# Selection of the second token half moved beside the feed-forward products, in 28 pieces

## The reference, cut to what matters

```python
inter = xf @ c1_w.T @ c2_w.T                # (tokens, 1792), rank 16
blk = inter.reshape(B * T, 56, 32)
idx = argmax(blk, -1) + arange(0, 1792, 32) # one unit of each 32
h = relu(einsum('bkm,bm->bk', w1[idx], xf))
out = einsum('bk,bkm->bm', h, w2t[idx])
```

## Time and profile before

| | |
|---|---|
| median of 3 runs | 2140.83 us (2140.81 to 2145.97) |
| the profiled execution's own time | 2140.16 us |
| its span | 2138.4 us |
| TensorE busy | 2061.0 us (96%) |
| VectorE busy | 1596.8 us (75%) |
| ScalarE busy | 1447.9 us (68%) |
| GpSimd busy | 773.9 us (36%) |
| 16 DMA engines | 20.9% of the span for the main queue |

### The profile page before, as it was taken

One profiled execution on the slowest core, in us unless ns is written; L12 is line 12 of the kernel. 1 busy time (PEld: TensorE's weight loads), 2 busy tenths in 40 slices (PEclk: granted clock), 3 DMA queues, 4 the chain that ended last, 5 costly groups with the idle time before them and its releaser, 6 DMA issues. The chain is left out here.

```text
span 2138.4 us, 33991 instructions
## 1 busy us (share of the span) xinstructions
PE 2061.0 (96%) x12990; PEld 1662.1 (78%) x12990; DVE 1596.8 (75%) x1763; ACT 1447.9 (68%) x3141; POOL 773.9 (36%) x423
## 2 busy tenths in 40 slices
PE   6899999999999999999999999997899989999988
PEld 5788888888888888888888888884587668888864
DVE  6778788878877877887888787787623358787774
ACT  4777786777777678677677778782633357777761
POOL 2244444444354436434454434534444201010101
PEclk8999999999999999999999999997999999999999
DMA  3222232222222222122222212221132111010001
GB/s 110 106 88 91 78 109 72 77 101 78 99 80 103 76 81 107 70 99 79 74 100 101 83 69 99 86 92 33 59 116 88 42 44 30 22 30 22 14 1 40
DMA packets 56241, 157.46 MB, mean 74 GB/s; under 512 B 16656, under 2 KB 27152, under 8 KB 47632
## 3 DMA queue, kind: packets, MB, share of 16 engines
q1 hardware_dynamic: 56080, 155.28, 20.9%
HBM read 152.64 MB, written 2.62 MB: 73 GB/s over the span
## 5 line engine op out<-in xcount | busy, mean ns | idle before, releaser
L610 PE MATMUL PS<-xnh,wh 128*128 128x512 f32 x1272 | 509.8, 401 | 8.6 <-DVE xnl L1590 5.8
L612 PE MATMUL PS<-xnh,wl 128*128 128x512 f32 x1272 | 497.0, 391 | 0.0
L611 PE MATMUL PS<-xnl,wh 128*128 128x512 f32 x1272 | 496.1, 390 | 0.0
L1627 DVE SCALAR_TENSOR_TENSOR arena<-PS,arena 128x1020 f32<-128x1020 f32 (+2 forms) x240 | 305.6, 1274 | 31.1 <-ACT arena L1219 25.4
L1180 ACT ACTIVATE PS<-x,arena 128x128 f32<-128x128 f32 x1024 | 308.1, 356 | 21.1 <-DVE arena L1659 20.1
L610 PEld LDWEIGHTS PS<-xnh,wh 128*128 128x128 f32 x1272 | 239.2, 188 | 63.3 <-issue 14.3
L450 POOL TENSOR_TENSOR zl<-arena,zh 128x1024 fp32r<-128x1024 f32 x63 | 176.8, 2807 | 293.6 <-ACT zh L1202 293.6
L612 PEld LDWEIGHTS PS<-xnh,wl 128*128 128x128 f32 x1272 | 239.2, 188 | 52.0
L611 PEld LDWEIGHTS PS<-xnl,wh 128*128 128x128 f32 x1272 | 239.5, 188 | 46.1
L446 POOL TENSOR_TENSOR arena<-arena 128x1024 f32<-128x1024 f32 x63 | 151.9, 2412 | 297.9 <-ACT arena L1198 297.9
L435 POOL TENSOR_TENSOR wl<-arena,wh 128x1024 fp32r<-128x1024 f32 x72 | 174.8, 2428 | 199.5 <-ACT wh L1169 199.5
(11 more groups left out here) (253 smaller groups left out, 4123.9 us busy)
## 6 DMA issues: line engine op xcount, KB each, us to landing
x<-decay SPq DMA_DIRECT2D x64, 1024.0 KB, 4.6
arena<-in_w_xg SPq DMA_DIRECT2D x72, 512.0 KB, 5.5
arena<-in_w_o SPq DMA_DIRECT2D x32, 512.0 KB, 3.4
arena<-in_w_f SPq DMA_DIRECT2D x28, 512.0 KB, 3.5
x<-in_x SPq DMA_DIRECT2D x3, 1024.0 KB, 5.4
arena<-in_w_h SPq DMA_DIRECT2D x16, 192.0 KB, 2.9
arena<-in_w_h SPq DMA_DIRECT2D x16, 129.0 KB, 2.8
out<-x SPq DMA_DIRECT2D x8, 256.0 KB, 2.0
```

What stands on the lines that cost most here:

```text
L610: mm(PS[:, bank], ah, bh, start=(n == 0), stop=False)
L611: mm(PS[:, bank], ah, bl, start=False, stop=False)
L612: last = mm(PS[:, bank], al, bh, start=False, stop=(n == len(terms) - 1))
L1627: ins = stt(o, pair_of(bank).rearrange("p q (b t) -> p q b t", t=SEQ)[:, :, :, :SEQ - k], w[:, 3 - k:4 - k], o, ALU.mult, ALU.add)
```

## The change

Only the 8 selection steps of tokens 0 to 511 stay ahead of the feed-forward loop. The selection of tokens 512 to 1023 is cut into 28 pieces j of 128 tokens by 2 tiles (256 units), spread over iterations n = 0 to 14: TensorE does step(2n) between hidden(n + 1) and down(n), and step(2n + 1) behind down(n). One step holds the two score products of piece j, the first-maximum product of piece j-2 and the two turns of piece j-1, in banks T and S. The score weights move from zl to woh and wol, so zl is free for the loop. hidden(1) moves ahead of the last first_part, and down(0) waits for the 8 masks of the first half. The low part of the input's second half becomes four operations in iterations 4 to 7 on GpSimd. The head weights and four small constants are loaded together behind w_f of n = 17, after a wait for all 36 masks.

The diff without the score weights' new place and the waits on it:

```diff
 NF = 2 * FT1
+NPC = FT1 // 2 * NU // 2
...
-        c2r = zl.rearrange("p k t -> p (k t)")[:, 0:F1]
+        c2r = [v.rearrange("p k t -> p (k t)")[:, 0:F1 // 2] for v in (woh, wol)]
...
+        def piece(j):
+
+            return j // 4, NU // 2 + j % 4
+
...
-            for n in range(NF):
-                if n >= 2:
-                    sp.wait_ge(s["fw2l"], n - 1)
-                sp.dma_start(w_f[:, n % 2], d["w_f"][n % FT1]).then_inc(s[f"w_f{n % 2}"], 16)
+            for m in range(NF):
+                if m >= 2:
+                    sp.wait_ge(s["fw2l"], m - 1)
+                sp.dma_start(w_f[:, m % 2], d["w_f"][m % FT1]).then_inc(s[f"w_f{m % 2}"], 16)
+                n = m
                 if n == 5:
-                    sp.wait_ge(s["mT"], 2 * NU)
+                    sp.wait_ge(s["c1_ps"], 2)
+                    sp.wait_ge(s["c2_r"], 3)
                     for dst, name in ((w_qc, "w_qc"), (w_kvc, "w_kvc"), (bq, "bq"), (bkv, "bkv"), (bv, "bv"), (bo, "bo"), (w_oT, "w_oT")):
                         sp.dma_start(dst, d[name]).then_inc(s["a_in"], 16)
+                if n == FT1 + 3:
+                    sp.wait_ge(s["mT"], NU + NPC)
                     for n in range(2):
                         sp.dma_start(bqB[n * QB:(n + 1) * QB], d["bq"][0:QB]).then_inc(s["a_in"], 16)
                         sp.dma_start(bias_rows[n * NPAIR:(n + 1) * NPAIR], d["w_hB"][:, QB, n]).then_inc(s["a_in"], 16)
-                if n in (6, 7):
-                    heads_load(n - 6)
+                    for i in range(2):
+                        heads_load(i)
...
-                po.wait_ge(s["ln_h"], h + 3)
-                nc.gpsimd.tensor_tensor(xnl[:, :, half(h)], xn[:, :, half(h)], xnh[:, :, half(h)].bitcast(F32), ALU.subtract)\
-                    .then_inc(s["ln_l"], 1)
+            po.wait_ge(s["ln_h"], 3)
+            nc.gpsimd.tensor_tensor(xnl[:, :, half(0)], xn[:, :, half(0)], xnh[:, :, half(0)].bitcast(F32), ALU.subtract)\
+                .then_inc(s["ln_l"], 1)
...
+                if 4 <= n < 4 + KD:
+                    po.wait_ge(s["ln_h"], 4)
+                    k = n - 4
+                    last = nc.gpsimd.tensor_tensor(xnl[:, k, half(1)], xn[:, k, half(1)], xnh[:, k, half(1)].bitcast(F32), ALU.subtract)
+                    if k == KD - 1:
+                        last.then_inc(s["ln_l"], 1)
...
-            for v in range(2 * NU):
-                if v == 2 * NU - 1:
-                    pe.wait_ge(s["ln_l"], 4)
+            def step(j):
+
+                if j == 0:
+                    pe.wait_ge(s["eqT"], NU)
+                    pe.wait_ge(s["t1"], 3)
+                if j < NPC:
+                    f, u = piece(j)
+                    pe.wait_ge(s["eq"], NU + j)
+                    for n in range(2):
+                        q, at = divmod(2 * f + n, FT1 // 2)
+                        last = mm(PS[:, T, col(n)], t1[:, col(u)], c2r[q][:, col(at)], start=True, stop=True)
+                    last.then_inc(s["in_ps"], 1)
+                if 2 <= j < NPC + 2:
+                    pe.wait_ge(s["eqT"], NU + j - 1)
+                    pe.wait_ge(s["mT"], NU + j - 2)
+                    mm(PS[:, S, SEQ:], ahead, eqT[:, j % 2, 0:2], start=True, stop=True).then_inc(s["first_ps"], 1)
+                if 1 <= j < NPC + 1:
+                    pe.wait_ge(s["eq"], NU + j)
+                    pe.wait_ge(s["eqT"], NU + j - 1)
+                    for n in range(2):
+                        last = nc.tensor.transpose(PS[:, S].bitcast(BF16)[:, col(n)], eq[:, (j - 1) % 2, col(n)], identB[:, :])
+                    last.then_inc(s["eqT_ps"], 1)
+
+            for v in range(NU):
+                if v == NU - 1:
+                    pe.wait_ge(s["ln_l"], 3)
                     hidden(0)
                 turn_part(v)
-                if v + 2 < 2 * NU:
+                if v + 2 < NU:
                     in_part(v + 2)
                 if v == 0:
                     c1_part(1, Y0, range(2, KD))
                 if v:
                     first_part(v - 1)
-            first_part(2 * NU - 1)
+            hidden(1)
+            first_part(NU - 1)
 
             for n in range(NF):
-                if n + 1 < NF:
+                if n + 1 == FT1:
+                    pe.wait_ge(s["ln_l"], 4)
+                if 0 < n < NF - 1:
                     hidden(n + 1)
+                if n <= FT1:
+                    step(2 * n)
                 if n == 0:
-                    pe.wait_ge(s["mT"], 2 * NU)
+                    pe.wait_ge(s["mT"], NU)
                 if n == FT1 + 1:
                     pe.wait_ge(s["x2"], 1)
                     narrow(T, 2 * P, onesD, x, 0).then_inc(s["ln_mean"], 1)
@@ -899,6 +946,8 @@
                     pe.wait_ge(s["rows_w"], 3)
                     widen_pair(1, sdn[:, col(2)]).then_inc(s["ln_rw"], 1)
                 down(n)
+                if n <= FT1:
+                    step(2 * n + 1)
 
 
             def latent_A(h, bank):
@@ -1368,20 +1417,35 @@
                     ac.wait_ge(s[done], n - 1)
                 act(wh[:, k, c], w_f[:, k, c], ACT.Copy).then_inc(s["fw2h" if part else "fw1h"], 1)
 
-            for v in range(2 * NU):
+            def high_half(h):
+                ac.wait_ge(s["ln_xn"], h + 3)
+                act(xnh[:, :, half(h)], xn[:, :, half(h)], ACT.Copy).then_inc(s["ln_h"], 1)
+
+            def step(j):
+                if 1 <= j < NPC + 1:
+                    ac.wait_ge(s["eqT_ps"], NU + j)
+                    if j >= 3:
+                        ac.wait_ge(s["first_ps"], NU + j - 2)
+                    act(eqT[:, (j - 1) % 2, 0:2], PS[:, S].bitcast(BF16)[:, 0:SEQ].rearrange("p (c t) -> p c t", t=P), ACT.Copy)\
+                        .then_inc(s["eqT"], 1)
+                if 2 <= j < NPC + 2:
+                    f, u = piece(j - 2)
+                    ac.wait_ge(s["first_ps"], NU + j - 1)
+                    act(maskT[:, 2 * f:2 * f + 2, col(u)], PS[:, S, SEQ:].rearrange("p (c t) -> p c t", t=P), ACT.Relu)\
+                        .then_inc(s["mT"], 1)
+
+            for v in range(NU):
                 turned_part(v)
                 if v == 0:
                     t1_high(1, Y0)
                 if v:
                     mask_part(v - 1)
-                if v in (4, 8):
-                    h = v // 4 - 1
-                    ac.wait_ge(s["ln_xn"], h + 3)
-                    act(xnh[:, :, half(h)], xn[:, :, half(h)], ACT.Copy).then_inc(s["ln_h"], 1)
-                if v in (10, 12):
-                    rounded(v // 2 - 5, 0, "h_ps")
-                    rounded(v // 2 - 5, 1, "f_out")
-            mask_part(2 * NU - 1)
+                if v == 1:
+                    high_half(0)
+                if v in (3, 5):
+                    rounded(v // 2 - 1, 0, "h_ps")
+                    rounded(v // 2 - 1, 1, "f_out")
+            mask_part(NU - 1)
 
             for n in range(NF):
                 if 1 <= n < NF - 1:
@@ -1390,8 +1454,16 @@
                 if n >= 2:
                     ac.wait_ge(s["f_out"], n - 1)
                 act(zh[:, n % 2, 0:HALF], hs[:, n % 2], ACT.Copy).then_inc(s["hs_h"], 1)
+                if 1 <= n <= FT1:
+                    step(2 * n - 1)
+                if n == 2:
+                    high_half(1)
                 if 1 <= n < NF - 1:
                     rounded(n + 1, 1, "f_out")
+                if n <= FT1:
+                    step(2 * n)
+                if n == FT1:
+                    step(2 * n + 1)
                 if n == FT1 + 2:
                     mean(2, 0, T, 2 * P)
                 if n == FT1 + 5:
@@ -1825,14 +1897,31 @@
                 tt(eq[:, q].rearrange("p (b g i) -> p b g i", b=2, i=SP1), scores, across(top.unsqueeze(3), shape),
                    ALU.is_equal).then_inc(s["eq"], 1)
 
+            def step(j):
+                if j >= NPC:
+                    return
+                scores = PS[:, T, 0:SEQ].rearrange("p (g i) -> p g i", i=SP1)
+                top = mx[:, j % 2, 0:SEQ // SP1]
+                ve.wait_ge(s["in_ps"], NU + j + 1)
+                V.tensor_reduce(top, scores, AX_X, ALU.max).then_inc(s["mx"], 1)
+                ve.wait_ge(s["mx"], NU + j + 1)
+                ve.wait_ge(s["eqT_ps"], NU + max(j - 1, 0))
+                tt(eq[:, j % 2, 0:SEQ].rearrange("p (g i) -> p g i", i=SP1), scores, across(top.unsqueeze(2), (P, SEQ // SP1, SP1)),
+                   ALU.is_equal).then_inc(s["eq"], 1)
+
             for n in range(NF):
                 k, h = n % 2, n // FT1
                 ve.wait_ge(s["h_ps"], n + 1)
                 if n >= 2:
                     ve.wait_ge(s["hs_l"], n - 1)
+                ve.wait_ge(s["mT"], NU + (n - FT1) // 2 * 4 + 4 if h else NU)
                 stt(hs[:, k], PS[:, A + k], 0.0, maskT[:, n % FT1, half(h)], ALU.max, ALU.mult).then_inc(s["hs"], 1)
                 ve.wait_ge(s["hs_h"], n + 1)
                 tt(zl[:, k, 0:HALF], hs[:, k], zh[:, k, 0:HALF].bitcast(F32), ALU.subtract).then_inc(s["hs_l"], 1)
```

(4 more changed lines are left out.)

16 lines of the change are left out of this document (10 added, 6 removed).

## The result

The changed kernel takes 2149.08 us (median of 20 runs, 2143.98 to 2151.86) against 2143.01 us for the kernel before on the same chip (20 runs, 2140.03 to 2146.56). The ratio is 1.0025, 95% interval 1.0019 to 1.0031: 5.4 us slower, 4.1 to 6.6 (the medians lie 6.1 apart), and within the 0.3% (6.4 us) that the prediction called the same.

What follows compares the result with a forecast made beforehand. TensorE was taken to bound the feed-forward loop and VectorE the last selection steps; -17.0 + 1.5 + 11.4 + 1.0 + 2.7 + 3.4 = +3.0 us gave a median of 2143.8 us, range 2137 to 2152.

Steps and rivals of the forecast that it cites:

- The case that the text called likeliest: The forecast itself for the whole kernel: 2143.8 us, told as the same within 0.3%; chance 0.52.
- Eight steps: Selection ahead of the loop: eight steps of 2.13 us removed, so the first hidden product starts earlier, -17.0 us.
- Start of the loop: From the first hidden product to down(0): 10.0 us against 8.5, with 3.3 us of TensorE waiting, +1.5 us.
- Pieces: Between down(0) and down(13): 26 steps of small TensorE products at 0.44 us each, +11.4 us (8.8 to 15.6).
- The upper bound: Cost of one step: about 0.6 us, with a first product's delay of 0.14 at each of two operand changes.
- Weight chain: In the loop, from a step's end to the low part of hidden(n + 2)'s weights: 3.1 us, covered by 3.16, 0.
- The rival of 2152 us: In the loop: GpSimd's low part begins 0.69 us late, weight chain 3.8 against 3.16 us, 8 us slower; chance 0.15.
- VectorE's low part beside GpSimd's: At the shared SBUF port: VectorE's low part waits for GpSimd's, started 0.6 us earlier, with over 2 us of room.
- Change of halves: From down(13)'s end to down(14): step(28) waits for VectorE's comparison of piece 27, 5.6 us against 4.59, +1.0 us.
- End of iteration 14: Ahead of hidden(16): ScalarE writes the last mask before rounding tile 16's weights, so TensorE waits, +2.7 us.
- SyncE's burst: Head weight loads of 8.7 us ahead of tile 18's w_f: 0.4 us late unless TensorE is delayed, 0.
- Clock: Behind the new pauses of 3.3 and 2.6 us: 3.4 us at 1.2 GHz each, costing 1.7 each, +3.4 us.

Runs made afterwards that it cites:

- The first experiment: Changed kernel with ScalarE's rounding of tile 16's first weights ahead of the last piece's mask; ratio 1.0017 to the kernel before.
- the filled pause: Changed kernel with 12 wide products, whose result nobody reads, in TensorE's pause ahead of down(0); ratio 1.0025 to the kernel before.
- the kernel with the low part whole: Changed kernel with the second half's low part as one GpSimd operation in iteration 4 instead of four; ratio 1.0033 to the kernel before.
- the kernel with four repairs: Changed kernel with tile 16's rounding first, head weights' loads spread, last first maximum ahead of hidden(1), one score product in 24 pieces; ratios 1.0000 and 0.9992 to before.

## Why the prediction was right

The forecast was 2143.8 against 2140.83, +3.0 us; it came to +5.4 (4.1 to 6.6) timed and +4.2 in the part of the trace that the change touches. The case that the text called likeliest is the one that happened, with its marks: the first down 15.9 us earlier, counted from the start of selection (15.5 forecast); idle of 3.12 us ahead of it, ended by the low part; an iteration of 6.47 us (6.3 forecast); hidden(16) released by GpSimd 2.6 us late; 3.4 us at half clock behind both; no idle TensorE time between steady iterations.

- **Eight steps**, -17.0: -17.7. The last eight steps before took 17.03 us, as the eight periods say; the other 0.65 is in the eight that stay (1487.72 to 1506.84, 19.12 us, against 18.47), and why was not looked into. It makes up for a part of what the pieces cost beyond the forecast; that is luck.
- **Start of the loop**, +1.5: +1.8; undoing its order gave 1.1 of it back.
- **Pieces**, +11.4 at 0.44: the mis-sized term, 13.2 at 0.51. The products' own spacings are less than forecast: 0.18 + 0.12 + 0.08 = 0.38 us. What the sum lacked is the 0.09 us that the first wide product behind a step takes longer, and the 0.004 us on each of the eleven others. The upper bound had the first of these, "the delay of a first product, 0.53 against 0.39 us", at two places of 0.14; it is one of 0.09. The kernel without pieces shows that all of it is theirs.
- **Weight chain**, 0, on a cover of 0.06 us: right, with 0.47 of room in fact, so the chain was sized 0.4 us too long. ScalarE's copy, mask and rounding start 0.28 and 0.26 us apart (1604.87, 1605.15, 1605.41), where I had taken 0.43 for each. The rival of 2152 us needs 0.5 us more in the chain than there is.
- **VectorE's low part beside GpSimd's**, predicted to be late and hidden: 1.14 us at 1593.89 instead of 0.69, ending 0.55 us behind GpSimd's operation from 1593.19 to 1594.48, and nobody waits for it. The rule of the Trainium skill that the prediction weighed (SBUF — State Buffer, "SBUF: two separate sides") agrees with this row.
- **Change of halves**, +1.0: +0.8. **End of iteration 14**, +2.7: +2.6, and 4.15 us came back, its clock with it, once two orders were mended.
- **SyncE's burst**, 0: right in the kernel after, and only because the end's pause hides it. The first experiment and the kernel without pieces show the wait (3.27 and 1.83 us).
- **Clock**, +3.4: right in both places, 1.7 us each; the filled pause shows the cause for the first. The argument was that each pause is longer than one of 2.33 us that had a fall behind it. It does not hold as a rule: behind the same 2.33 us ahead of hidden(16) no fall came in the kernel with the low part whole, so this half of the term was in part luck. The reason I gave for leaving out the change of halves (a pause of 1.70 us ahead of down(14) had no fall behind it) was weak: with the same waits a fall came there in two other kernels.

What the prediction did not see is that the time at half clock in the rest of the program, whose code is untouched, differs from kernel to kernel and need not be the same in two executions. In the profile of the kernel after this was 0.85 us; in others it was larger than the effect that was looked for.

## What to carry to other kernels

Work put into a stage that TensorE bounds is paid in TensorE's time: 0.51 us a step, 28 times, against 17 us won, so before moving idle engines' work, price the products that it brings, their number as well as their columns, and what they do to the products behind them. When a pause is removed, look at once at the queue that it had been hiding (here SyncE's burst), and take both away together. And measure an edit by the stage it touches as well as by the whole: falls of the clock elsewhere moved the rest of this program by up to 5 us from that of the kernel before, so a gain of 2 us is hardly to be seen, or refuted, in the total. One profile is one execution; read the clock of all timed ones beside it.

## What the runs showed of the hardware

- The granted clock's falls depend on more than the length of a pause: 1.93 us ahead of the scores was followed by 3.4 us at 1.2 GHz in the kernel with four repairs (0.57 over 1706 to 1710) and by none before (1.00 over 1708 to 1712); the change of halves had a fall in two kernels of nine with nearly the same waits (1.0 to 1.1 and 0.5 to 0.6 us); the 2.33 us ahead of hidden(16) had one in the kernel after and none in that with the low part whole. In two kernels profiled twice the falls from selection on came at the same places, moved with the kernel's start; ahead of selection they differed (37.6 and 47.8 us at half clock for the four repairs), and the mean clock of that kernel's executions lay between 0.980 and 0.988.
- Of small products between wide ones, two of 128 columns took 0.18 us (0.06 and 0.12), one of 256 took 0.12, and two bf16 turns of 128 took 0.08; half of a wide product's 0.227 is 0.113. The first wide product behind them took 0.32.
- Behind the five small products of a step wide ones ran at 0.231 us, behind four or six at 0.227 (3.24, 3.14 and 3.31 us from step to step), but at 0.232 also behind a pause of 1.70 us with no small product.
- Short operations of ScalarE on 256 elements last 0.38 us each but start 0.28 us apart, so a chain of them is shorter than the sum of its durations.
